# Ten state buffers instead of nine in a fused Mamba and convolution kernel, with the engines' written orders laid out anew

## The chip, the cores and the metric

The kernel runs on one core of a Trainium2 chip. The metric is the device time of one execution in microseconds. Before the change, three runs took 858.09, 858.99 and 859.21 us; the median is 858.99.

## What is computed

The input x has the shape (4, 128, 32, 32), float32. Two Mamba blocks read it as 128 sequences of 32 tokens with 128 features, both in the same memory order. For each block:

```
xc, z  = split(x @ W_in.T)                 # 2 x 256 features
xc     = silu(causal_conv4(xc) + conv_b)
dt,B,C = softplus(W_dt(...) + b_dt), 16 rows B, 16 rows C from W_x(xc)
h[n]   = exp(dt * A[n]) * h[n] + dt * xc * B[n]       # n = 0..15, along the 32 tokens
y      = (sum_n h[n] * C[n] + D * xc) * silu(z)
out    = y @ W_out.T
```

Then y1 + y2 + x goes through batch norm, relu, a 3x3 convolution with binarised weights, batch norm, relu, a second such convolution, and is added to the block's input.

## The kernel before, in words

The tokens are cut into chunks of 512. Four images, two chunks each, two Mambas: 16 items, in each of which the 16 states of the recurrence are worked off one after the other. A state is a tile of 128 partitions x 2 halves x 512 tokens. The whole loop is software-pipelined by hand: each engine has a loop over items k (from -1) and over slots s = 0..15, and at each slot it runs what tables at the top of the file (lines 51 to 96) name. The numbers in the tables are states; 16 and above are states of the next item, and below 0 of the item before. Nothing else orders the work but these tables and semaphores.

One state n passes through these steps:

- A decay exp(dt*A) is made by ScalarE in two halves. Plain states (PLAIN) have it written into one of two pairs of PSUM banks, pair n % 2 (plain_decays, line 654). Turned states (TURNED) have it written into the state's SBUF slot (turned_decays, line 665).
- The input dt*xc*B. For plain states GpSimd multiplies u by a row of B spread over the partitions, into the state's slot (times_b, line 565). For turned states ScalarE makes four products with tokens on partitions (line 678; three such buffers), and TensorE transposes them, eight instructions, into the pair (turn_input, line 1051).
- VectorE scans (line 865). The target is the slot if GpSimd multiplies by C next (POOL_C, line 574), else the pair, and VectorE itself multiplies by C into the slot (DVE_C, line 875).
- TensorE sums the slot into y_sum (line 1058). Then the slot is free.

A pair of banks is free again after the scan two states before, or after VectorE's C product if that state was in DVE_C. A slot is n % SLOTS, and is free once state n - SLOTS is summed (wait_slot_free). The last columns of the slots hold raw weights in the set-up, so some slots also wait for these to be transposed.

In the same slots each engine prepares the next item: TensorE the taps of the causal convolution (PE_TAPS), z (PE_Z), dbc (PE_DBC), dt (PE_DT), the transposes of B and u (PE_B_TOK, PE_U_TOK); ScalarE xc, gate, dbc, dt and copies (ACT_XC and so on), with a load of its function tables in four places; GpSimd u (POOL_U). VectorE gates the sums of the item before inside state 4 (DVE_POST, line 887). From the second image on, the output projection of the image before (PE_OUT, line 1150) is added in (DVE_OUT, line 898) in two items of each image; in the last item, projections are early (AT_EARLY_OUT, AT_EARLY_ADD). The 3x3 kernels are signed, transposed and summed in slots AT_KERNELS of the first item. SyncE issues the loads that spread the rows of B and C (store_rows, spread_b, spread_c).

Below, s4 is the scan of state 4, C4 its C product, B4 and T4 its input by GpSimd or its transposed input, P4 its products, d4 and td4 its decay (plain or turned). Items are counted from 0. The loop is followed by the two convolutions, which run alone.

Of the kernel before, what the change touches and what calls it, by code (L numbers as in the profile page):

```python
# [41 lines left out]
PART = NB * H * PADDED + 2  # L42
WCOUNT = C * C * TAPS

SLOTS = 9
PAIRS = 2
PRODUCTS = 3
FAR = 1e33
# [2 lines left out]

TURNED = (1, 3, 6, 7, 10, 13, 14, 15)
PLAIN = tuple(s for s in range(NST) if s not in TURNED)
POOL_C = (0, 1, 2, 3, 7, 8, 10, 12, 14, 15)
DVE_C = tuple(s for s in range(NST) if s not in POOL_C)
B_GROUPS = ((0,), (2,), (4, 5), (8, 9), (11, 12))
C_GROUPS = tuple((s, s + 1) for s in range(0, NST, 2))

PE_TAPS = {13: ((2, 0),), 14: ((2, 1),), 1: ((1, 2), (1, 3)), 3: ((1, 4), (1, 5), (1, 6), (1, 7))}
PE_OUT = {8: (0,), 10: (1, 2), 11: (3,)}
PE_TURNS = {1: (3,), 4: (6,), 5: (7,), 8: (10,), 11: (13,), 12: (14,), 13: (15,), 15: (17,)}
PE_SUMS = {0: (-4, -3), 2: (-2,), 3: (-1,), 4: (0,), 6: (1, 2), 8: (3, 4), 9: (5,), 10: (6, 7), 11: (8,), 12: (9,),
           13: (10,), 15: (11,)}
POOL_B = {0: (4,), 1: (5,), 5: (8, 9), 8: (11, 12), 12: (16,), 13: (18,)}
ACT_DECAYS = {1: (2,), 3: (4,), 4: (5,), 7: (8,), 8: (9,), 9: (11,), 10: (12,), 15: (16,)}  # L70
ACT_TURNED = {2: (3, 6), 4: (7,), 8: (10,), 9: (13,), 13: (14,), 14: (15, 17)}
ACT_EARLY = {6: (13,), 13: (15,), 15: (17,)}
ACT_PRODUCTS = {3: (7,), 4: (10,), 12: (14,), 15: (19, 22)}
PE_Z = 4
PE_DBC = 6
PE_DT = 7
PE_B_TOK = 9
PE_U_TOK = (11, 12)
ACT_XC = 4
ACT_GATE = 6  # L80
ACT_DBC = 7
ACT_DT = 8
ACT_B_TOK = 12
ACT_U_TOK = (13, 14)
POOL_U = 8

LATE_SUMS = sum(e < 0 for states in PE_SUMS.values() for e in states)
DVE_POST = 4
DVE_OUT = 13

POST_INSIDE = True
AT_KERNELS = (8, 9, 10)
AT_STATS = 8
AT_EXACT = (11, 12)
AT_EARLY_OUT = (5, 6, 8, 9)
# [8 lines left out]
def by_pool(n):  # L104

    return n % NST in POOL_C and n != LAST - 1

# [9 lines left out]
def mamba_conv_kernel(nc, t, out):  # L117
# [3 lines left out]
    with ctx:  # L121
# [10 lines left out]

        state = sb("state", [128, SLOTS, HALVES, CHUNK])
        raw = state[:, :, :, :].rearrange("p a h n -> p (a h n)")
        raw_free = [SLOTS * HALVES * CHUNK]

# [175 lines left out]
        def wait_slot_free(eng, n):  # L312

            wait(eng, summed, n - SLOTS + 1)
            if RAW_SLOT <= n < SLOTS:
                eng.wait_ge(setup_mm, WEIGHT_GROUPS)
# [22 lines left out]
        def tile(n):  # L339
            return state[:, n % SLOTS, :, :]  # L340

# [115 lines left out]
        @block.sync  # L457
        def _(sp):
            load_w_in(sp, 0)
            load_w_x(sp, 0)  # L460
            load_x_tokens(sp, 1)
            load_w_in(sp, 1)
            load_conv_w(sp, 1)
            load_x_tokens(sp, 2)
            load_w_x(sp, 1)
            load_vectors(sp, 1)
            load_w_dt(sp, 1)
            load_a_log(sp, 1)
            for m in range(2):
                load_w_out(sp, m)  # L470

            def load_kernels():

                for n in range(2):
                    sp.dma_start(k_raw[n], t[f"L1_conv_w{n}"].rearrange("o i a b -> o (i a b)")).then_inc(load_k, 16)
                    sp.dma_start(gamma[n][:, :], t[f"L1_conv_gamma{n}"].rearrange("(p a) -> p a", a=1)).then_inc(load_k, 16)
                    sp.dma_start(beta[n][:, :], t[f"L1_conv_beta{n}"].rearrange("(p a) -> p a", a=1)).then_inc(load_k, 16)

            def store_rows(k):

                if k >= 2:
                    for q in range(len(B_GROUPS)):
                        sp.wait_ge(b_loaded[q], 16 * (k - 1))
                    for q in range(len(C_GROUPS)):
                        sp.wait_ge(c_loaded[q], 16 * (k - 1))
                sp.wait_ge(dbc_ready, k + 1)
                sp.dma_start(bc_rows[k % 2], dbc[0:BC, :]).then_inc(rows_stored, 16)
                sp.wait_ge(rows_stored, 16 * (k + 1))

            def spread(wide, first, k, row, count, loaded):  # L490

                sp.dma_start(wide[:, first:first + count, :].rearrange("p s n -> p (s n)"),
                             bc_rows[k % 2][row:row + count, :].rearrange("s n -> (s n)").unsqueeze(0)
                             .to_broadcast([128, count * CHUNK])).then_inc(loaded, 16)

            def spread_b(k, q):

                states = B_GROUPS[q]
                if k > 0:
                    sp.wait_ge(plain_input, before(PLAIN, NST * (k - 1) + states[-1] + 1))  # L500
                spread(b_wide, PLAIN.index(states[0]), k, states[0], len(states), b_loaded[q])

            def spread_c(k, q):

                if k > 0:
                    for s in C_GROUPS[q]:
                        wait_output(sp, NST * (k - 1) + s)
                spread(c_wide, C_GROUPS[q][0], k, NST + C_GROUPS[q][0], len(C_GROUPS[q]), c_loaded[q])

            for k in range(ITEMS):  # L510
                store_rows(k)
                spread_b(k, 0)
                spread_b(k, 1)
                spread_b(k, 2)
                spread_c(k, 0)
                spread_b(k, 3)
                spread_c(k, 1)
                spread_c(k, 2)
                spread_b(k, 4)
                spread_c(k, 3)  # L520
                spread_c(k, 4)
                spread_c(k, 5)
                spread_c(k, 6)
                spread_c(k, 7)
                if k == 0:
                    load_kernels()
                if k % ITEMS_PER_IMAGE == ITEMS_PER_IMAGE - 1:
                    b = k // ITEMS_PER_IMAGE
                    sp.wait_ge(z_mm, 2 * (k + 1))
                    sp.dma_start(res[b], x[b].rearrange("c h w -> c (h w)")).then_inc(load_res[b], 16)  # L530

            for n in range(TILES):
                sp.wait_ge(y_ready, n + 1)
                b, half = n // 2, n % 2
                sp.dma_start(out[b].rearrange("c h w -> c (h w)")[:, half * CHUNK:(half + 1) * CHUNK],
                             res_half(n)).then_inc(y_stored, 16)
            sp.wait_ge(y_stored, 16 * TILES)
# [81 lines left out]
        def _(act):  # L619
# [26 lines left out]
            def plain_decays(n):  # L646

                if n >= LAST or n % NST in TURNED:
                    return
# [18 lines left out]
            def products(n):  # L668
# [3 lines left out]
                k, s = n // NST, n % NST  # L672
                j = before(TURNED, n)
                wait(act, u_tok_ready, 2 * k + 2)
# [13 lines left out]
            def prepare(k, s):  # L688
# [23 lines left out]
                if s == ACT_DT:  # L712
                    act.preload_act_table_set("softplus")  # L713
                    wait(act, plain_decay, HALVES * len(PLAIN) * (k - 1))
                    wait(act, turned_decay, HALVES * len(TURNED) * (k - 1))
                    for h in range(HALVES):
# [538 lines left out]
```

## Time and profile before

| | us |
|---|---|
| median of three runs | 858.99 |
| the profiled execution, its time | 859.51 |
| its span | 857.6 |
| TensorE (PE) busy | 760.1 (89%) |
| VectorE (DVE) busy | 757.2 (88%) |
| ScalarE (ACT) busy | 724.1 (84%) |
| GpSimd (POOL) busy | 710.3 (83%) |

The shares are means over stages with different limits: the set-up until 42.12 us, the loop until about 768.5 us, and the convolutions until the end, where GpSimd does nothing and VectorE and ScalarE wait for TensorE. An instruction's duration is a little more than the distance to the next one's start, since neighbours overlap: a scan lasts 2.26 us. Busy TensorE is not TensorE at its peak.

### The profile page before, as it was taken

To read this page: it belongs to the slowest core of one execution; us is meant where nothing else is said; L and a number is where in the kernel's file an instruction comes from. 1 tells how busy PE (TensorE), PEld (TensorE's weight loads), DVE (VectorE), ACT (ScalarE), POOL (GpSimd) and SP (SyncE) were. 2 spreads that over 40 slices of the span, in tenths; PEclk is the share of its full clock that TensorE was granted. 3 is DMA by queue.
4 is the path that set the end of the run, shared out by engine and by line. 5 is a ranking of instruction groups with operands and counts; after the bars stand their busy time and mean duration, and the time that the engine had idled before them with its cause. 6 is when DMAs were issued, how large, how long until landed. Compare 5 with 4: busy or idle time off the path is not lost.

```text
span 857.6 us, 13007 instructions
## 1 busy us (share of the span) xinstructions
PE 760.1 (89%) x4470; PEld 380.3 (44%) x4470; DVE 757.2 (88%) x482; ACT 724.1 (84%) x1295; POOL 710.3 (83%) x335
## 2 busy tenths in 40 slices
PE   7786989999899999898999998989999986868988
PEld 3533434343445353344353533434534433426866
DVE  2698999999999999999999999999999999984141
ACT  3788999999999999999999999999999999435050
POOL 0477899999999999999999999999999999940000
PEclk9699999999999999999999999999999998898999
DMA  5717143253525151617070717271525244000011
GB/s 141 285 68 249 50 151 148 113 210 105 194 78 216 70 209 48 250 58 265 28 270 26 257 42 248 75 247 50 228 72 195 104 158 165 1 1 1 0 37 62
DMA packets 39146, 110.97 MB, mean 129 GB/s; under 512 B 7244, under 2 KB 9384, under 8 KB 39080
## 3 DMA queue, kind: packets, MB, share of 16 engines
q1 hardware_dynamic: 37724, 109.84, 36.3%
q8 instruction: 36, 0.59, 0.3%
q10 hardware_dynamic: 1356, 0.29, 0.2%
q14 instruction: 30, 0.25, 0.1%
HBM read 106.97 MB, written 3.15 MB: 128 GB/s over the span
## 4 chain that ended last, share of the span: by engine, by line
DVE 33%; issue 20%; ACT 18%; PE 17%; POOL 11%; DMA 0%; ACTq 0%; DVEq 0%; POOLq 0%
DVE state L865 15%; DVE bank L865 12%; PE bank L1225 8%; POOL state L574 5%; ACT bank L654 5%; ACT product L678 5%; POOL state L565 5%; ACT state L665 3%; PE bank L1058 3%; DVE state L875 2%; PE bank L1051 2%; ACT dt L718 1%; ACT L713 1%; PE bank L1037 1%; PE bank L991 1%
## 5 line engine op out<-in xcount | busy, mean ns | idle before, releaser
L574 POOL TENSOR_TENSOR state<-state,wide 128x1024 f32<-128x1024 f32 x159 | 373.0, 2365 | 21.8 <-DVE state L865 21.8
L565 POOL TENSOR_TENSOR state<-u,wide 128x1024 f32<-128x1024 f32 x128 | 301.7, 2369 | 8.2 <-PE bank L1058 8.2
L1058 PE MATMUL bank<-state,ident 64*64 64x512 f32 x2048 | 263.7, 625 | 1.0 <-POOL state L574 0.9
L865 DVE TENSOR_TENSOR_SCAN state<-state,bank 128x1024 f32<-128x1024 f32 x95 | 214.7, 2270 | 1.0 <-PE bank L1051 1.0
L678 ACT ACTIVATE product<-u_tok,b_tok 128x256 f32<-128x256 f32 x512 | 212.4, 496 | 2.3 <-PE bank L1051 1.8
L1051 PE MATMUL bank<-ident,product 128*128 128x128 f32 x1024 | 142.0, 283 | 70.4 <-ACT product L678 26.2
L654 ACT ACTIVATE bank<-dt,a_neg 128x512 f32<-128x512 f32 x256 | 165.5, 677 | 30.4 <-DVE state L865 17.1
L1051 PEld LDWEIGHTS bank<-ident,product 128*128 128x128 f32 x1024 | 114.5, 144 | 166.3 <-issue 91.8
L665 ACT ACTIVATE state<-dt,a_neg 128x512 f32<-128x512 f32 x256 | 166.5, 710 | 0.2 <-PE bank L1058 0.2
L865 DVE TENSOR_TENSOR_SCAN bank<-bank,state 128x1024 f32<-128x1024 f32 x64 | 146.1, 2282 | 1.1 <-ACT bank L654 0.3
L865 DVE TENSOR_TENSOR_SCAN state<-bank,state 128x1024 f32<-128x1024 f32 x64 | 145.2, 2268 | 0.0
L875 DVE TENSOR_TENSOR state<-bank,wide 128x1024 f32<-128x1024 f32 x97 | 118.6, 1223 | 9.3 <-DVE bank L865 1.0
L1037 PE MATMUL bank<-x_t,w_tap 128*128 128x512 f32 x256 | 124.5, 620 | 0.0
L1058 PEld LDWEIGHTS bank<-state,ident 64*64 64x64 f32 x2048 | 67.3, 136 | 114.0 <-issue 107.5
L1225 PE MATMUL bank<-wide 128*128 128x512 f32 (+1 forms) x288 | 71.2, 411 | 8.0 <-ACT u_tok L775 4.0
L865 DVE TENSOR_TENSOR_SCAN bank<-state,bank 128x1024 f32<-128x1024 f32 x33 | 75.2, 2280 | 0.5 <-ACT state L665 0.5
L1037 PEld LDWEIGHTS bank<-x_t,w_tap 128*128 128x128 f32 x256 | 46.1, 194 | 65.3 <-issue 65.3
L1225 PEld LDWEIGHTS bank<-wide 128*128 128x128 f32 x288 | 57.2, 199 | 21.8 <-ACT wide L775 4.4
L587 POOL TENSOR_TENSOR u<-dt,xc 128x1024 f32<-128x1024 f32 x16 | 37.8, 2360 | 25.6 <-ACT dt L718 23.1
L1110 PE MATMUL bank<-dbc,w_dt 8*128 8x512 f32 x64 | 31.7, 613 | 0.5 <-ACT dbc L621 0.5
L1083 PE MATMUL bank<-x_t,w_z 128*128 128x512 f32 x64 | 30.3, 594 | 0.6 <-ACT xc L700 0.6
L1100 PE MATMUL bank<-xc,w_x 128*40 128x512 f32 x64 | 30.6, 600 | 0.0
(93 smaller groups left out, 493.9 us busy)
## 6 DMA issues: line engine op xcount, KB each, us to landing
wide<-bc_rows SPq DMA_DIRECT2D x176, 512.0 KB, 6.8
wide<-bc_rows SPq DMA_DIRECT2D x32, 256.0 KB, 3.6
x_t<-in_x_dram SPq DMA_DIRECT2D x4, 512.0 KB, 4.8
out_dram<-x_t SPq DMA_DIRECT2D x8, 256.0 KB, 2.0
k_room<-in_L_conv_w_dram SPq DMA_DIRECT2D x2, 576.0 KB, 13.0
bc_rows<-dbc SPq DMA_DIRECT2D x16, 64.0 KB, 1.6
state<-in_L_conv_W_in_dram SPq DMA_DIRECT2D x2, 256.0 KB, 3.9
x_tok<-in_x_dram ACTq DMA_DIRECT2D x1, 256.0 KB, 3.7
```

The source lines that it names most:

```text
L565: pool.tensor_tensor(tile(n), u[:, :, :], over_halves(b_wide[:, PLAIN.index(s), :]), ALU.mult).then_inc(plain_input, 1)
L574: pool.tensor_tensor(tile(n), tile(n), over_halves(c_wide[:, n % NST, :]), ALU.mult).then_inc(output_pool, 1)
L587: pool.tensor_tensor(u[:, :, :], dt[m][:, :, :], xc[m][:, :, :], ALU.mult).then_inc(u_ready, 1)
L654: act.activation(pair[n % PAIRS][:, h, :], dt[k % 2][:, h, :], ACT.Exp, scale=a_neg[k % 2][:, h, s:s + 1]).then_inc(plain_decay, 1)
L665: act.activation(tile(n)[:, h, :], dt[k % 2][:, h, :], ACT.Exp, scale=a_neg[k % 2][:, h, s:s + 1]).then_inc(turned_decay, 1)
L678: act.activation(product[j % PRODUCTS][:, blk, :], u_tok[:, blk, :], ACT.Identity, scale=b_tok[k % 2][:, blk, s:s + 1]).then_inc(product_r ...
L865: dve.tensor_tensor_scan(flat(target), flat(decay), flat(source), 0.0, ALU.mult, ALU.add).then_inc(scanned, 1)
L875: dve.tensor_tensor(tile(n), pair[n % PAIRS], over_halves(c_wide[:, s, :]), ALU.mult).then_inc(output_dve, 1)
L1037: mm = pe.matmul(by_sequence(work[h]), w_tap[k % 2][:, h, tap, :], chunk_of(k, tap), start=(tap == 0), stop=(tap == KCONV - 1))
L1051: mm = pe.transpose(pair[n % PAIRS][:, h, 128 * blk:128 * blk + 128], product[j % PRODUCTS][:, blk, 128 * h:128 * h + 128], ident[:, :])
L1058: return pe.matmul(y_sum[64 * h:64 * h + 64, b, :], weights[rows, :], source[rows, h, :], start=first, stop=last)
L1225: mm = pe.matmul(by_row(bank[n])[:, dst, :], k_exact[layer][:, q, :], shifted(part, q)[:, src, 0:W], start=(q == TAP_ORDER[0] and part == ...
```

## The change

SLOTS goes from 9 to 10. The sets of turned states and of states whose C product is GpSimd's are changed; each keeps its size (8 and 10). All tables of orders are rewritten, and one SyncE load is moved.

```diff
-SLOTS = 9
+SLOTS = 10
-TURNED = (1, 3, 6, 7, 10, 13, 14, 15)
+TURNED = (1, 2, 5, 6, 10, 13, 14, 15)
-POOL_C = (0, 1, 2, 3, 7, 8, 10, 12, 14, 15)
+POOL_C = (1, 2, 3, 5, 6, 7, 10, 12, 14, 15)
-B_GROUPS = ((0,), (2,), (4, 5), (8, 9), (11, 12))
+B_GROUPS = ((0,), (3, 4), (7, 8), (9,), (11, 12))
-PE_TAPS = {13: ((2, 0),), 14: ((2, 1),), 1: ((1, 2), (1, 3)), 3: ((1, 4), (1, 5), (1, 6), (1, 7))}
-PE_OUT = {8: (0,), 10: (1, 2), 11: (3,)}
-PE_TURNS = {1: (3,), 4: (6,), 5: (7,), 8: (10,), 11: (13,), 12: (14,), 13: (15,), 15: (17,)}
-PE_SUMS = {0: (-4, -3), 2: (-2,), 3: (-1,), 4: (0,), 6: (1, 2), 8: (3, 4), 9: (5,), 10: (6, 7), 11: (8,), 12: (9,),
-           13: (10,), 15: (11,)}
-POOL_B = {0: (4,), 1: (5,), 5: (8, 9), 8: (11, 12), 12: (16,), 13: (18,)}
-ACT_DECAYS = {1: (2,), 3: (4,), 4: (5,), 7: (8,), 8: (9,), 9: (11,), 10: (12,), 15: (16,)}
-ACT_TURNED = {2: (3, 6), 4: (7,), 8: (10,), 9: (13,), 13: (14,), 14: (15, 17)}
-ACT_EARLY = {6: (13,), 13: (15,), 15: (17,)}
-ACT_PRODUCTS = {3: (7,), 4: (10,), 12: (14,), 15: (19, 22)}
+PE_TAPS = {14: ((2, 0), (2, 1)), 2: ((1, 2), (1, 3), (1, 4), (1, 5), (1, 6), (1, 7))}
+PE_OUT = {9: (0, 1), 12: (2,), 13: (3,)}
+PE_TURNS = {0: (1,), 1: (2,), 3: (5,), 5: (6,), 8: (10,), 12: (13,), 13: (14,), 14: (15,)}
+PE_SUMS = {0: (-2,), 2: (-1,), 5: (0, 1), 6: (2, 3), 8: (4, 5), 9: (6,), 10: (7, 8), 11: (9,), 12: (10,), 13: (11,),
+           15: (12, 13)}
+POOL_B = {1: (7, 8), 5: (9,), 8: (11,), 10: (12,), 11: (16,), 12: (19,), 13: (20,)}
+ACT_DECAYS = {0: (3,), 3: (4,), 5: (7,), 6: (8,), 7: (9,), 8: (11,), 9: (12,), 14: (16,)}
+ACT_TURNED = {0: (5,), 3: (6,), 7: (10,), 9: (13,), 11: (14, 15), 12: (17,), 13: (18,)}
+ACT_EARLY = {0: (6,), 11: (15,), 15: (17, 18, 21)}
+ACT_PRODUCTS = {3: (10,), 6: (13,), 8: (14,)}
-PE_DBC = 6
-PE_DT = 7
-PE_B_TOK = 9
-PE_U_TOK = (11, 12)
-ACT_XC = 4
-ACT_GATE = 6
-ACT_DBC = 7
-ACT_DT = 8
-ACT_B_TOK = 12
-ACT_U_TOK = (13, 14)
-POOL_U = 8
+PE_DBC = 5
+PE_DT = 6
+PE_B_TOK = 11
+PE_U_TOK = (12, 14)
+ACT_XC = 3
+ACT_GATE = 4
+ACT_DBC = 5
+ACT_DT = 7
+ACT_B_TOK = 10
+ACT_U_TOK = (11, 14)
+POOL_U = 10
-DVE_OUT = 13
+DVE_OUT = 14
-AT_KERNELS = (8, 9, 10)
+AT_KERNELS = (9, 10, 11)
@@ the loads of an item, on SyncE
                 spread_c(k, 2)
+                spread_c(k, 3)
                 spread_b(k, 4)
-                spread_c(k, 3)
                 spread_c(k, 4)
```

With these sets VectorE makes the C products of states 0, 4, 8, 9, 11 and 13, where it made those of 4, 5, 6, 9, 11 and 13. PE_Z, DVE_POST, AT_EARLY_OUT and AT_EARLY_ADD are unchanged.

## Rows read from the trace of the kernel before

**Rows 1.** Busy time by stretch: length, busy time (instructions) per engine, TensorE's clock.

```profile
42.12:93.66 51.54, 40.51 (x222) 19.72 (x221) 46.62 (x30) 44.92 (x77) 38.25 (x18) 0.90 0.43 148
93.66:716.32 622.66, 574.81 (x3550) 263.42 (x3548) 613.74 (x343) 604.09 (x1093) 618.78 (x281) 0.98 0.41 146
716.32:768.50 52.18, 36.09 (x264) 17.58 (x264) 49.69 (x34) 29.84 (x56) 42.04 (x21) 0.90 0.06 23
137.79:181.93 44.14, 40.30 (x240) 17.05 (x240) 43.56 (x26) 43.12 (x80) 43.44 (x20) 0.96 0.36 138
```

**Rows 2.** VectorE in one middle item: start, duration, line, operation, shapes.

```profile
139.97 2.26 DVE L865 TENSOR_TENSOR_SCAN state<-state,bank 128x1024 f32<-128x1024 f32 x1
146.51 2.27 DVE L865 TENSOR_TENSOR_SCAN bank<-bank,state 128x1024 f32<-128x1024 f32 x1
151.01 2.29 DVE L865 TENSOR_TENSOR_SCAN bank<-bank,state 128x1024 f32<-128x1024 f32 x1
...
154.54 2.29 DVE L865 TENSOR_TENSOR_SCAN bank<-state,bank 128x1024 f32<-128x1024 f32 x1
```

**Rows 3.** VectorE in the first item; in brackets the idle time before, and its releaser.

```profile
77.51 0.35 DVE L845 COPY k_t<-bank 128x128 bf16<-128x128 bf16 x2 [2.54 <-PE bank L1012]
...
88.97 2.29 DVE L865 TENSOR_TENSOR_SCAN state<-state,bank 128x1024 f32<-128x1024 f32 x1 [0.84 <-PE bank L1051]
```

**Rows 4.** VectorE in the last item.

```profile
725.04 2.27 DVE L865 TENSOR_TENSOR_SCAN bank<-bank,state 128x1024 f32<-128x1024 f32 x1
...
739.58 0.69 DVE L898 TENSOR_TENSOR x_t<-x_t,bank 128x512 f32<-128x512 f32 x1 [0.70 <-PE bank L1150]
...
750.53 0.69 DVE L898 TENSOR_TENSOR x_t<-x_t,bank 128x512 f32<-128x512 f32 x1 [1.17 <-PE bank L1150]
```

**Rows 5.** GpSimd, the multiplications of two neighbouring items that make u.

```profile
257.34 2.36 POOL L587 TENSOR_TENSOR u<-dt,xc 128x1024 f32<-128x1024 f32 x1 [0.17 <-POOL state L565]
...
301.80 2.37 POOL L587 TENSOR_TENSOR u<-dt,xc 128x1024 f32<-128x1024 f32 x1 [0.17 <-POOL state L565]
```

**Rows 6.** ScalarE in one middle item, in order of time.

```profile
148.57 1.32 ACT L665 ACTIVATE state<-dt,a_neg 128x512 f32<-128x512 f32 x2
...
151.21 1.27 ACT L700 ACTIVATE xc<-bank,vectors 128x512 f32<-128x512 f32 x2
...
155.55 1.06 ACT L686 ACTIVATE gate<-bank 128x512 f32<-128x512 f32 x2
...
158.25 1.30 ACT L654 ACTIVATE bank<-dt,a_neg 128x512 f32<-128x512 f32 x2 [0.33 <-DVE state L875]
...
178.06 0.58 ACT L621 ACTIVATE u_tok<-bank 128x512 f32<-128x512 f32 x1
178.67 1.70 ACT L678 ACTIVATE product<-u_tok,b_tok 128x256 f32<-128x256 f32 x4
180.28 1.28 ACT L654 ACTIVATE bank<-dt,a_neg 128x512 f32<-128x512 f32 x2
181.51 3.29 ACT L678 ACTIVATE product<-u_tok,b_tok 128x256 f32<-128x256 f32 x8
```

**Rows 7.** TensorE: transposed inputs in a middle and the last item, then two windows.

```profile
151.23 1.07 PE L1051 MATMUL bank<-ident,product 128*128 128x128 f32 x8 [0.56 <-DVE state L875]
...
729.77 1.94 PE L1051 MATMUL bank<-ident,product 128*128 128x128 f32 x8 [5.91 <-DVE state L875]
...
729.77:733.60 3.83, 3.83 (x20) 2.29 (x24) 3.73 (x3) 1.96 (x5) 3.83 (x3) 0.50 0.00 0
...
163.60:167.20 3.60, 3.60 (x19) 0.81 (x17) 3.50 (x3) 3.56 (x5) 3.13 (x2) 0.53 0.69 264
```

**Rows 8.** ScalarE in the first item: signs of the kernels, first copy of them.

```profile
63.99 2.20 ACT L640 ACTIVATE k_room<-k_room 128x1152 bf16<-128x1152 f32 x2
...
72.54 1.02 ACT L621 ACTIVATE k_t<-bank 128x1024 bf16<-128x1024 bf16 x1
```

**Rows 9.** The page's DMA issues: size, median us from issue to landing.

```profile
wide<-bc_rows SPq DMA_DIRECT2D x176, 512.0 KB, 6.8
```

## The prediction

> **What bounds the kernel now.** I read the windows by stretch first, then VectorE (DVE) in order of time, then who waits for whom. The state loop runs from 42.12 us, where the first scan starts, to 768.5 us: 16 items of 16 states. In its 14 middle items (93.66 to 716.32) DVE is busy 613.74 of 622.66 us, GpSimd (POOL) 618.78 and ScalarE (ACT) 604.09 [rows 1]. Three engines run level, so a gain for one is worth only what it lacks to the next.
>
> DVE has the floor. Inside an item scans start 2.18 us apart (s0 of one item at 137.79, s1 at 139.97); a scan whose C product is also DVE's takes 3.53 (151.01 to 154.54); the state that also holds the gating takes 4.50 (146.51 to 151.01) [rows 2]. An item has ten, five and one of these: 21.80 + 17.65 + 4.50 = 43.95 us. The item of 137.79 took 44.14 [rows 1]. Six of the 14 middle items also add an output (0.60). The floor of the stretch is 14 x 43.95 + 6 x 0.60 = 618.9, so only 3.8 us of its 622.66 are idle. The first item takes 51.54, with visible waits of 2.54 (for the kernel transposes of state 10) and 0.84 (turned input of state 14) [rows 3]; the last takes 52.18 with waits of 0.70 and 1.17 for early output projections [rows 4]. What an order can win is these waits, under 10 us in all.
>
> POOL's own pace: one u to the next, 257.34 to 301.80, is 44.46 us with nothing idle [rows 5]. That is level with DVE's 622.66 / 14 = 44.48.
>
> **The change, counted.** Turned states stay 8, POOL's C products 10, DVE's 6, the table loads, transposes and the loads of rows as many as before (those of B are regrouped, five either way). So no engine gets less work; only waits can go or come. I walk the new orders with the starts of the rows.
>
> *Scans and pairs.* DVE's C set has 0 in place of 5 and 8 in place of 6; state 4 stays in it, so the floor stays 43.95. New starts inside an item, from s0 = 0: s1 3.53, s2 5.71, s3 7.89, s4 10.07, s5 14.57, s6 16.75, s7 18.93, s8 21.11, s9 24.64, s10 28.17, s11 30.35, s12 33.88, s13 36.06, s14 39.59, s15 41.77.
>
> *Middle items, ACT.* A decay of a plain state can start only when the scan two before has left the pair. ACT's run from the next item's d0 (0.17 after s15 starts, as the pair's release comes some 0.1 after a scan's end) to its d7 has no idle place. Steps from the rows: decay 1.23; copy of u and a product 2.22, further products 1.61; a turned decay with a table load 2.64; xc and two products 4.34, so xc alone 1.12; gate with a table load 2.37 (155.55 to 158.25, less the wait of 0.33) [rows 6]. The run is 0.17 + 1.23 (d0) + 2.22 (u, P1) + 4.83 (P2, P5, P6) + 3.69 (d3, td5, d4) + 2.64 (td6, load) + 1.12 (xc) + 1.61 (P10) + 2.37 (gate, load) + 1.30 (d7) + 0.10 (its signal) = 21.28. DVE needs from s15 to s7 2.18 + 18.93 = 21.11. So s7 waits some 0.15 in an item that follows one without an addition; the addition, now between s14 and s15, gives ACT 0.60 and hides it. Eight items x 0.15 = 1.2. With 0.03 per item of uneven starts: 1.7 us where 3.8 are idle today. Term: -2.0. Bounds: -3.8 (no waits at all) and +1.0 (a TensorE transposition late once per plain item by 0.35, see below). I take -2.0, since each step is a row of this same stage.
>
> *Middle items, TensorE and POOL.* The turned inputs must land in 2.1 us between the release of their pair and the scan (states 2, 6, 13, 15), and a transposition takes 1.07 [rows 7]; in the walk the margins are 0.85, 0.6, 0.85 and 0.75, and in items with outputs 0.1 to 0.9. POOL does C5, C6, C7 at 16.2, 18.5, 20.9 plus its lag x; they need s5 to s7 ended, so x is at least 0.57, and B11 must end before 30.35, so x at most 4.8. At 44.46 against DVE's (618.9 + 1.7) / 14 = 44.33 the lag grows by 1.8 in 14 items: POOL stays inside. The tenth slot is what permits B7, B8 at the item's start: they need states 13 and 14 summed, and by nine slots 14 and 15.
>
> *SyncE's queue.* The load of C rows 6 and 7 now stands ahead of that of B rows 11 and 12. It waits for C7 (done at 23.2 + x), the other for B12 (27.9 + x), both long before the next item's use; a load lands in 6.8 us [rows 9]. Cost 0; if C7 were late by a whole product (2.3), the next item's B11, due 25 us after its s0, would still be served. At the start the second B load is twice as large, and its rows are wanted by POOL 2.3 us after the first; a late landing eats only idle time of POOL.
>
> *First item.* s0 stays at 42.12 (setup copies on DVE). C0 moves to DVE, so s1 starts at 45.65. ACT waits for scan 1 to end (47.9) for d3, then its run to d7 ends at 60.9, while s7 would be due at 60.1: about 0.9 lost. The signs of the kernels (2.20 [rows 8]) now stand behind dt, d11 and P14: d7's start at 59.5 + 1.23 + copy 0.5 + d8 1.23 + P13 1.61 + d9 1.23 + 2.64 + dt 1.15 + load 1.3 + d11 1.23 + P14 1.61 = 73.4, signs until 75.6; d12, td13, then the copy of kernel 0 (1.02 [rows 8]) until 79.2; transposes of kernel 1, its copy until 81.6; the sums reach DVE at 82.2. DVE is there at 78.5: the wait is 3.7, not 2.54. But T14 and T15 now have their pairs in time (wait 0.84 and a smaller one go). s0 of the next item comes at 93.5 against 93.66. Term: -0.1; bounds -3.4 (both waits of before gone) and +0.8 (TensorE still slow at T15, as at T14 before). I take -0.1, the walk.
>
> *Last item.* The early projections keep their slots (5, 6, 8, 9) and additions theirs (after s7 and s10). In front of the first addition TensorE runs T6, the skip and sum of 0, then outputs, two sums, outputs. Before, T6 started 4.73 after s4 (725.04 to 729.77) and the addition ran 9.81 later (739.58) [rows 4, 7]. Now T6 waits for the C product of state 4, again 4.73 after s4, which starts at 10.07 and not at 8.72; the work behind it is the same (T7 leaves, sum 3 comes in, both near 1 us). The addition comes at 10.07 + 4.73 + 9.81 = 24.6; DVE is there at 21.1, not 22.6. The wait is 3.5 instead of 0.70. The second addition keeps its distance (T10 waits for C8, but DVE has that product in its path too): 1.2. Term: +2.8. [...]
>
> [...]
>
> **Sum.** -2.0 - 0.1 + 2.8 = +0.7. The profiled execution: span 857.6, its time 859.5; hence 860.2. The median of the runs shown lies 0.5 below that execution, so I predict 859.7. Under 0.2% (1.7 us) a measurement of this kernel can't tell from no change.
>
> **Rivals.**
> - *The first item pays.* The extra slot lets POOL multiply B7 and B8 while it idles today, and the wait for the kernels' sums closes as well: -3.4 instead of -0.1, in all 2.8 - 2.0 - 3.4 = -2.6, and 859.0 - 2.6 = 856.4. For it: POOL's spare time there, and that ACT idles in that item. Against: the signs' place behind dt. Chance 0.28, faster.
> - *POOL sets the pace.* If its lag starts above 4 us, DVE follows at 44.46 per item and the -2.0 falls away: +2.7, 861.7. For it: 618.78 of 622.66 us busy. Against: my walk starts it at 0.6. Chance 0.12, slower.
> - *ACT's run from d0 to d7.* It holds gate, xc and seven decays and products without a gap. If it takes 0.4 more than 21.28, by the gate's wait for z behind a late xc, say, each of the 8 plain items pays it at s7: +3.2, in all +3.9: 862.9. It decides from 21.1 us on (21.7 after an addition). For it: ACT works 43.1 of 44.14 [rows 1]. Against: every step is a row's. Chance 0.20, slower.
>
> The forecast has 0.40. Faster 0.28, same 0.40, slower 0.32. Range: from 856.0 (the first rival, a little beyond) to 863.2 (the last with its price).
>
> **What would show it.** Middle item without addition 44.1 to 44.2, with addition 44.6, and 620 to 621 for fourteen. In the first item a wait of 3 to 4 us for the transposes of the kernels and one near s7. In the last, a wait of 2 to 3.5 us before the first addition. Idle time of POOL between its first B products and C1 near 7.7 us. It is wrong if the 14 items take over 622, or if the wait before the first addition is under 1 us.

## The result and the profile after

The kernel with ten buffers takes 862.30 us (median of 20 executions, 858.36 to 864.59); the kernel before took 858.35 (20 executions, 855.88 to 859.65) beside it. The ratio is 1.0048 [1.0037, 1.0059]: slower by 0.48%. The forecast was 859.7 from a median of 858.99: a sum of +0.7, which it called no measurable change, in a range of 856.0 to 863.2. The time is in the range, but the change is +3.95, clear of the noise and more than five times the sum. The profiled execution took 863.14 us with a span of 861.3 (before: 859.51 and 857.6).

The 20 executions of the kernel after fall into two groups. Four, whose mean granted TensorE clock was 0.966 to 0.974, took 858.36 to 859.47; the other sixteen, at 0.958 to 0.962, took 860.82 to 864.59. The profile is one of the sixteen, and none of the four was kept. So the loss read below is that of most executions, and a part of it comes and goes.

Windows of the kernel after, by stretch: start and end, length, then per engine busy time (instructions) of TensorE, its weight loads, VectorE, ScalarE and GpSimd, then the granted clock.

```profile
42.34:95.64 53.30, 40.44 (x243) 18.96 (x245) 46.92 (x29) 42.49 (x71) 37.23 (x17) 0.94 0.44 150
95.64:717.30 621.66, 568.59 (x3560) 268.07 (x3552) 613.74 (x344) 603.14 (x1093) 618.06 (x281) 0.98 0.43 147
717.30:773.23 55.93, 38.03 (x240) 19.32 (x240) 49.95 (x34) 30.35 (x59) 38.99 (x20) 0.82 0.06 20
773.23:861.30 88.07, 75.34 (x332) 60.35 (x328) 28.46 (x48) 22.91 (x34) 0.00 (x0) 0.95 0.07 24
```

Set against [rows 1]:

| stretch | before | after | difference | predicted |
|---|---|---|---|---|
| until the first scan | 42.12 | 42.34 | +0.2 | 0 |
| first item | 51.54 | 53.30 | +1.8 | -0.1 |
| 14 middle items | 622.66 | 621.66 | -1.0 | -2.0 |
| last item, to the convolutions | 52.18 | 55.93 | +3.7 | +2.8 |
| convolutions | 89.10 | 88.07 | -1.0 | 0 |

The sum is the +3.7 by which the spans differ. VectorE's 613.74 us of work in the middle items is the same to the last digit: no work went, only waits did. The convolutions are the same program; they were granted 0.95 of the clock here and 0.94 before.

Of these differences the -1.0 of the middle items is the least certain, since it is one execution against one. In seven profiles of kernels with the new order (the one after and the runs below that leave these items alone) the 14 items take 621.08 to 623.07 us, 621.7 in the mean; in four with the old order 622.21 to 624.13, 623.2 in the mean. So -1.5 is the better figure. Single items ran longer where the granted clock was lower: in the run with the later additions the item at 137.17 took 45.18 us at 0.92 and the next 44.16 at 1.00; in the kernel after the items of this kind at 139.91, 184.17 and 361.83 took 44.26 to 44.27 at 0.96.

*The first item.* VectorE in the kernel after, in order of time (start, duration, line, operation, shapes, and in brackets the idle time before it with its releaser):

```profile
61.10 2.29 DVE L865 TENSOR_TENSOR_SCAN state<-bank,state 128x1024 f32<-128x1024 f32 x1 [0.55 <-ACT bank L654]
...
77.45 1.23 DVE L875 TENSOR_TENSOR state<-bank,wide 128x1024 f32<-128x1024 f32 x1
83.80 0.36 DVE L845 COPY k_t<-bank 128x128 bf16<-128x128 bf16 x2 [5.12 <-PE bank L1012]
84.07 0.15 DVE L848 TENSOR_SCALAR k_mean<-bank 128x2 f32<-128x2 f32 x1
84.25 1.39 DVE L851 TENSOR_TENSOR k_mean_sq<-k_mean 128x2 f32<-128x2 f32 x1
```

State 7 waits 0.55 for ScalarE's decay. Then VectorE stands 5.12 us until the 3x3 kernels' sums are ready, where [rows 3] had 2.54 in the same place. ScalarE and TensorE of the same stretch:

```profile
73.51 2.20 ACT L640 ACTIVATE k_room<-k_room 128x1152 bf16<-128x1152 f32 x2
...
78.07 1.00 ACT L621 ACTIVATE k_t<-bank 128x1024 bf16<-128x1024 bf16 x1
...
82.06 0.22 ACT L621 ACTIVATE b_tok<-bank 128x64 f32<-128x64 f32 x1 [2.99 <-PE bank L1114]
82.18 1.02 ACT L621 ACTIVATE k_t<-bank 128x1024 bf16<-128x1024 bf16 x1
```

```profile
75.86 1.04 PE L1005 MATMUL bank<-k_room 128*128 128x128 bf16 x8 [5.00 <-ACT k_room L640]
76.83 3.69 PE L1058 MATMUL bank<-state,ident 64*64 64x512 f32 x16
80.45 1.07 PE L1005 MATMUL bank<-k_room 128*128 128x128 bf16 x8
...
83.42 0.34 PE L1012 MATMUL bank<-k_abs,k_room 128*128 128x2 f32 x2
```

TensorE has stood 5.00 us for the signs. From 75.90 to 81.50 it was busy all the time and the window was granted 0.50: the sums of two states (x16) take 3.69 us, where the same group takes 1.95 in a profile that was granted 1.00 there (both edits, below). The low and the high level of the clock are, in what follows, these two, a granted 0.50 and a granted 1.00. The second kernel's transposes start when these sums end, at 80.45, not when the first kernel's copy does, at 79.1. ScalarE's copy of the second kernel (82.18) also stands behind its copy of B (82.06), which waits 2.99 us for TensorE.

*The last item.* VectorE after, the rows that answer to [rows 4], and TensorE ahead of the first addition:

```profile
723.78 2.29 DVE L865 TENSOR_TENSOR_SCAN state<-state,bank 128x1024 f32<-128x1024 f32 x1 [0.69 <-PE bank L1051]
...
737.14 2.27 DVE L865 TENSOR_TENSOR_SCAN state<-bank,state 128x1024 f32<-128x1024 f32 x1
742.94 0.69 DVE L898 TENSOR_TENSOR x_t<-x_t,bank 128x512 f32<-128x512 f32 x1 [3.54 <-PE bank L1150]
...
755.21 0.69 DVE L898 TENSOR_TENSOR x_t<-x_t,bank 128x512 f32<-128x512 f32 x1 [1.13 <-PE bank L1150]
```

```profile
721.71 1.97 PE L1051 MATMUL bank<-ident,product 128*128 128x128 f32 x8
...
728.40 1.94 PE L1051 MATMUL bank<-ident,product 128*128 128x128 f32 x8 [3.70 <-DVE state L865]
732.89 1.94 PE L1051 MATMUL bank<-ident,product 128*128 128x128 f32 x8 [2.56 <-DVE state L875]
734.76 1.99 PE L1058 MATMUL bank<-xc,d_diag 64*64 64x512 f32 x8
```

The wait for the first addition is 3.54 (0.70 before), for the second 1.13 (1.17). A third wait, 0.69 at state 2, is new: T2 is the group at 721.71 and takes 1.97 us at a granted 0.54. T5 (728.40 to 731.00) and T6 with the skip's sum (732.89 to 736.80) were granted 0.50.

*The middle items.* VectorE at states 5, 6 and 7 of an item that follows one without an addition (184.17), and of one that follows one with an addition (273.19):

```profile
198.79 4.46 DVE L865 TENSOR_TENSOR_SCAN state<-state,bank 128x1024 f32<-128x1024 f32 x2
203.28 2.29 DVE L865 TENSOR_TENSOR_SCAN state<-bank,state 128x1024 f32<-128x1024 f32 x1
...
287.76 4.46 DVE L865 TENSOR_TENSOR_SCAN state<-state,bank 128x1024 f32<-128x1024 f32 x2
292.13 2.27 DVE L865 TENSOR_TENSOR_SCAN state<-bank,state 128x1024 f32<-128x1024 f32 x1
```

State 7 starts 4.49 after state 5 in the one and 4.37 in the other: a wait of 0.12, for the decay at the end of ScalarE's run. Items without an addition took 43.97 to 44.27 us, those with one 44.57 to 45.12.

### The profile page after: what moved, and what is told of

Same layout as the page of the kernel before. It is cut to its first block, busy times and chain, and to the rows that moved or that the text cites. A ratio compares the mean times of both kernels' runs of the same rounds, so it can differ in the third digit from the quotient of the medians.

```text
span 861.3 us, 13008 instructions
## 1 busy us (share of the span) xinstructions
PE 754.6 (88%) x4470; PEld 385.0 (45%) x4470; DVE 757.9 (88%) x482; ACT 722.3 (84%) x1295; POOL 710.2 (82%) x335
## 4 chain that ended last, share of the span: by engine, by line
DVE 45%; issue 23%; PE 15%; POOL 9%; ACT 7%; DMA 0%; DVEq 0%; ACTq 0%; POOLq 0%
DVE state L865 23%; DVE bank L865 16%; PE bank L1225 8%; POOL state L574 5%; POOL state L565 4%; DVE state L875 3%; PE bank L1037 2%; ACT state L665 1%; PE bank L1058 1%; ACT bank L654 1%; ACT product L678 1%; PE bank L991 1%; DVE x_tok L887 1%; PE bank L1051 1%; POOL u L587 1%
## 5 line engine op out<-in xcount | busy, mean ns | idle before, releaser
L1058 PE MATMUL bank<-state,ident 64*64 64x512 f32 x2048 | 259.5, 614 | 2.2 <-POOL state L574 2.2
L865 DVE TENSOR_TENSOR_SCAN state<-state,bank 128x1024 f32<-128x1024 f32 x111 | 249.1, 2273 | 0.7 <-PE bank L1051 0.7
L1051 PE MATMUL bank<-ident,product 128*128 128x128 f32 x1024 | 145.6, 288 | 57.3 <-DVE state L875 42.1
L1051 PEld LDWEIGHTS bank<-ident,product 128*128 128x128 f32 x1024 | 119.8, 148 | 145.7 <-issue 103.6
L865 DVE TENSOR_TENSOR_SCAN bank<-bank,state 128x1024 f32<-128x1024 f32 x80 | 182.4, 2280 | 0.0
L1037 PE MATMUL bank<-x_t,w_tap 128*128 128x512 f32 x256 | 119.5, 609 | 2.9 <-DVE x_t L898 2.9
L865 DVE TENSOR_TENSOR_SCAN state<-bank,state 128x1024 f32<-128x1024 f32 x48 | 109.2, 2275 | 0.8 <-ACT bank L654 0.5
L587 POOL TENSOR_TENSOR u<-dt,xc 128x1024 f32<-128x1024 f32 x16 | 37.8, 2363 | 25.8 <-ACT dt L718 23.2
L865 DVE TENSOR_TENSOR_SCAN bank<-state,bank 128x1024 f32<-128x1024 f32 x17 | 38.8, 2280 | 0.0
```

What stands on the lines that cost most here:

```text
L587: pool.tensor_tensor(u[:, :, :], dt[m][:, :, :], xc[m][:, :, :], ALU.mult).then_inc(u_ready, 1)
L865: dve.tensor_tensor_scan(flat(target), flat(decay), flat(source), 0.0, ALU.mult, ALU.add).then_inc(scanned, 1)
L1037: mm = pe.matmul(by_sequence(work[h]), w_tap[k % 2][:, h, tap, :], chunk_of(k, tap), start=(tap == 0), stop=(tap == KCONV - 1))
L1051: mm = pe.transpose(pair[n % PAIRS][:, h, 128 * blk:128 * blk + 128], product[j % PRODUCTS][:, blk, 128 * h:128 * h + 128], ident[:, :])
L1058: return pe.matmul(y_sum[64 * h:64 * h + 64, b, :], weights[rows, :], source[rows, h, :], start=first, stop=last)
```

## The experiments

Theory: the last item pays because VectorE comes earlier to an addition that TensorE cannot serve earlier, and the first because the signs of the kernels stand late and TensorE, which has stood 5.00 us for them, then works at a granted 0.50 (that the standing lowers the clock is my supposition); the middle items give a little, as the walk said. Of the runs, the ratios are to the kernel before, which took 858.14 to 858.37 (medians of 9 to 35 executions).

**The two early additions one slot later** (kernel after).

```diff
-AT_EARLY_ADD = (7, 10)
+AT_EARLY_ADD = (8, 11)
```

> The changed kernel with the two early additions after states 8 and 11 instead of 7 and 10; nothing else. Theory (the last item's additions cost time because VectorE reaches them 3.5 and 1.1 us before TensorE's output projections are ready): the waits of 3.54 and 1.13 us fall under 0.3 each, since VectorE now has 4.1 us more work (state 8 with its C product) before the first. The last item shortens by 4 to 4.6 us and the median falls by about 4, to 858.3. Rival (the wait only moves: what stands behind the additions, the transposition for state 10 and the second pair of projections, is what sets the item's length): both waits go but the scans behind them wait as long, and the time stays within 1 us of the changed kernel's 862.3.

Measured: 857.51 us (12 executions), ratio 0.9994 [0.9983, 1.0006]; 4.8 less than the kernel after. VectorE around the first addition:

```profile
737.07 2.27 DVE L865 TENSOR_TENSOR_SCAN bank<-bank,state 128x1024 f32<-128x1024 f32 x1
739.45 1.23 DVE L875 TENSOR_TENSOR state<-bank,wide 128x1024 f32<-128x1024 f32 x1
740.59 0.68 DVE L898 TENSOR_TENSOR x_t<-x_t,bank 128x512 f32<-128x512 f32 x1
```

The addition now stands behind state 8 and its product and waits for nothing; from the last item's first scan to its last it takes 47.4 us where it took 52.3. The expectation holds, and its rival is out. The waits of the last two additions, after the loop, are 2.7 us in both kernels, so nothing was only moved.

**The same edit in the kernel before.**

> The kernel before with its early additions after states 8 and 11. Theory: its waits of 0.70 and 1.17 us go, the last item shortens by 1.9 us, the ratio to before is 0.997 to 0.999. Rival (VectorE is not what ends that item): ratio 1.000 within 0.0005.

Measured: 856.28 (12), ratio 0.9978 [0.9968, 0.9988]: 2.1 less. The two waits of [rows 4] are worth 1.9. So the same slots cost the new order 4.8 and the old one 2.1: 2.7 us of what the change lost hang on the additions' slots.

**The kernels' transposes earlier in TensorE's and ScalarE's orders, and their sums later** (kernel after).

```diff
-AT_KERNELS = (9, 10, 11)
+AT_KERNELS = (8, 9, 13)
...
-                    pe.wait_ge(k_copied, s - AT_KERNELS[0])
+                    pe.wait_ge(k_copied, AT_KERNELS.index(s))
```

> The changed kernel with the 3x3 kernels' preparation in slots 8, 9 and 13 of the first item instead of 9, 10 and 11: signs right behind dt, the two copies one slot earlier, the last transposes, the sums and VectorE's reading of them behind state 13. Theory (the first item lost 1.8 us because the signs stand behind two more ScalarE steps, and VectorE reads the sums at state 11): VectorE's wait of 5.12 us disappears; the transposition for state 13 comes at 81 to 82 us, so 0.3 to 1.5 us of wait at s13 take its place; item 1 starts at 91.0 to 92.5 instead of 95.64, and the median falls by 3 to 4.5, to about 858.5. Rival (the wait covers other late work, for instance the transposed inputs of states 14 and 15 or GpSimd's products for the next item, which would hold VectorE next): item 1 still starts at 94 or later.

Measured: 860.94 (10), ratio 1.0032 [1.0019, 1.0045]; only 1.4 less, and the two intervals overlap. The wait for the sums fell from 5.12 to 0.24, but another came:

```profile
81.71 2.30 DVE L865 TENSOR_TENSOR_SCAN bank<-state,bank 128x1024 f32<-128x1024 f32 x1 [2.99 <-PE bank L1051]
...
85.57 0.35 DVE L845 COPY k_t<-bank 128x128 bf16<-128x128 bf16 x2 [0.24 <-PE bank L1012]
```

State 13 waits 2.99 us for its transposed input, which is queued behind the kernels' transposes and the sums of two states (1.07 and 3.69 us again, at a granted 0.50 from 74 to 79 us). What the expectation took for a freed wait was shared with the next thing in TensorE's queue. The next item does start at 92.12, inside what was expected, but only because the first scan came early (39.78, not 42.34; the set-up is the same code): the first item takes 52.34 where it took 53.30, which is the rival's side.

**Both edits.**

> The changed kernel with both earlier edits: additions after states 8 and 11, kernels in slots 8, 9 and 13. Theory (the two places are independent and add): the additions gave 4.6 us and the kernels' slots about 1.4, so the median is 856 to 857 and the ratio to before 0.997 to 0.999. Rival (with TensorE's phases shifted the late transposition at state 13 eats the second gain): within 0.5 us of the first edit alone, 857.5.

Measured: 856.84 (11), ratio 0.9986 [0.9975, 0.9997]; 5.5 less than the kernel after, where the two alone give 4.8 and 1.4. It is 0.7 less than with the additions alone, and those two intervals overlap: what the kernels' slots give is small, and not shown clear of the noise. In this profile the same TensorE code ran at a granted 1.00 from 74 to 79 us, and the wait at state 13 is 0.47:

```profile
74.11 0.70 PE L1005 MATMUL bank<-k_room 128*128 128x128 bf16 x8 [1.94 <-ACT k_t L621]
74.74 1.95 PE L1058 MATMUL bank<-state,ident 64*64 64x512 f32 x16
```

```profile
79.20 2.29 DVE L865 TENSOR_TENSOR_SCAN bank<-state,bank 128x1024 f32<-128x1024 f32 x1 [0.47 <-PE bank L1051]
```

Nothing in the first item differs between these two kernels, and ScalarE's starts agree to 0.02 us until 76.4; TensorE had stood 3.04 us for the signs in both, and was granted 0.50 after it in the one (70.49 to 72.00) and 1.00 in the other (70.47 to 72.10). What differs is the clock, and with it go the 2.5 us at state 13. At the high level this first item takes 49.84 us, 1.7 less than before.

**TensorE kept busy while it waits** (kernel after). Extra matmuls whose results nobody reads, in the first item ahead of the wait for the signs, and in slots 2 and 3 of the last. One wait is added, for a dt that was made in the item before.

```diff
+FILL_FIRST = 4
+FILL_LAST = {2: 3, 3: 2}
...
+            def fill(calls):
+                for _ in range(calls):
+                    pe.matmul(work[0][:, :], w_tap[0][:, 0, 0, :], w_tap[0][:, 0, :, :].rearrange("p k e -> p (k e)"))
...
                     pe.wait_ge(dt_ready, HALVES + 1)
+                    fill(FILL_FIRST)
                     pe.wait_ge(k_signed, 2)
...
+                    if k == ITEMS - 1 and s in FILL_LAST:
+                        wait(pe, dt_ready, HALVES * ITEMS)
+                        fill(FILL_LAST[s])
```

> The changed kernel with idle TensorE kept busy in two places by matmuls whose result nobody reads: four 128x512 ones in the first item while it waits for the signs of the kernels, three and two in the last item before the transpositions for states 5 and 6. No other edit. [...] Together 3 us less, a median near 859.5. Rival (the order alone makes the waits, the clock is incidental): both waits stay within 0.5 us of 5.12 and 3.54.

Measured: 860.30 (12), ratio 1.0025 [1.0012, 1.0038]; 2.0 less, with more work. Its lines are 2 (VectorE) and 8 (TensorE) higher. TensorE in the first item and at T6 and the skip's sum of the last:

```profile
74.18 0.71 PE L1013 MATMUL bank<-k_room 128*128 128x128 bf16 x8 [1.28 <-ACT k_room L642]
74.82 1.95 PE L1066 MATMUL bank<-state,ident 64*64 64x512 f32 x16
...
730.96 1.06 PE L1059 MATMUL bank<-ident,product 128*128 128x128 f32 x8 [1.71 <-DVE state L877]
731.95 1.09 PE L1066 MATMUL bank<-xc,d_diag 64*64 64x512 f32 x8
```

```profile
80.38 0.35 DVE L847 COPY k_t<-bank 128x128 bf16<-128x128 bf16 x2 [3.29 <-PE bank L1020]
...
738.95 0.69 DVE L900 TENSOR_TENSOR x_t<-x_t,bank 128x512 f32<-128x512 f32 x1 [1.59 <-PE bank L1158]
```

1.95 in place of 3.69, 1.06 in place of 1.94, 1.09 in place of 1.99. The wait for the kernels' sums becomes 3.29 (3.3 to 3.8 were expected), the one before the first addition 1.59 (1.6 to 2.2). TensorE was granted 1.00 in both stretches (69 to 79 us and 729 to 735), so these are the waits at the high level: the first near the 3.7 of the prediction, the second 1.95 below the 3.54 at the low level. Of the two waits' 8.66 us, 3.8 (1.83 and 1.95) go with the clock. Only 2.0 of them show in the time, where 3 were expected. That the extra matmuls are what kept the clock up is not shown by one profile: with both edits the stretch from 66 to 79 us was granted 1.00 without them. In this profile the second addition waits 1.73 and not 1.13, and the 14 middle items take 623.07 and not 621.66; two scans there wait 0.6 and 0.9 us for transposed inputs.

**The diagonal of the second Mamba made by ScalarE** (kernel after). Before the first scan VectorE writes two diagonals, which take 4.66 us beside GpSimd's products (the last section has the rows), and TensorE's transposes of x stand for VectorE's next copy (w_out).

```diff
                                 setup_copy(act, copy, g, setup_act)
+                        act.wait_ge(twin_ready, 2)
+                        act.wait_ge(*copied(11))
+                        act.wait_ge(diag_ready, HALVES)
+                        for h in range(HALVES):
+                            act.activation(d_diag[1][:, h, :], ident2[:, :], ACT.Identity,
+                                           scale=d_skip[1][:, h:h + 1]).then_inc(diag_ready, 1)
...
-            skip_diagonal(1)
             copies(GROUPS_AT_B_TOK)
```

> The changed kernel with the two set-up diagonals of the second Mamba written by ScalarE instead of VectorE. In all profiles VectorE's diagonal takes 0.25 us while GpSimd is idle, and 2.39 each while GpSimd multiplies; the first scan follows VectorE's set-up work. Theory (VectorE and GpSimd exclude each other there, and VectorE is the chain to the first scan): the first scan starts 3.5 to 4.6 us earlier against the same set-up phase (37.8 to 38.8 where it was 42.3), ScalarE adds 0.5, and the median falls by 2 to 4 to about 859. Rival (transposes of x or the first decay hold the first scan anyway): it starts less than 1 us earlier, no change in the median.

Measured: 859.31 (12), ratio 1.0015 [1.0003, 1.0027]; 3.0 less. TensorE in the kernel after, then in this one:

```profile
36.26 5.31 PE L991 MATMUL bank<-ident,x_tok 128*128 128x128 f32 x24 [2.08 <-DVE w_out L455]
```

```profile
33.67 5.11 PE L996 MATMUL bank<-ident,x_tok 128*128 128x128 f32 x24
```

The first scan starts at 39.42, not 42.34; 37.8 to 38.8 were expected. That start is no evidence by itself, since one set-up code gave 39.77 to 42.34 in different executions. But here the two set-ups are alike: their first eight matmuls of the causal convolution take 5.97 and 5.88 us. Where these take 3.70, the diagonal moves the first scan from 39.77 (both edits) to 37.84 (both and the diagonal, below).

**Nine buffers under the new order**, and **ten under the old one**.

```diff
-SLOTS = 10
+SLOTS = 9
```

> The changed kernel with nine state buffers again and all new orders kept. Theory (the buffer itself is worth little: the B products of states 7 and 8 then wait for the sums of states 14 and 15 of the item before, which comes out as GpSimd being 1 to 2 us later against VectorE, inside the window of about 4 us that it has): the 14 middle items take 621 to 623 us, as with ten, and the median stays within 1.5 us of the changed kernel's. Rival (the tenth buffer is what carries the new order): GpSimd idles in each item, an item takes 45 to 46 us, and the time rises by 10 us or more.

> The kernel before with ten state buffers and none of the new orders. Theory (in it only GpSimd waits for a buffer, 8.2 us, nearly all in the first and last item, and no other engine waits for GpSimd there): these waits of GpSimd shrink, VectorE's do not, and the median stays within 0.1% of before, 857.5 to 859.2. Rival (the buffers bound the start of the loop, so the buffer alone is worth 2 us or more): below 856.5. Second rival (moving everything behind the states by 4 KB per partition costs by itself): above 860.

Measured: nine buffers in the kernel after take 908.82 us (5), ratio 1.0572 [1.0551, 1.0593]; ten in the kernel before 858.14 (11), ratio 0.9999 [0.9989, 1.0009]. The first expectation's theory fell: 46.5 us more than the kernel after, where 1.5 at most were expected; its rival holds. The second's theory holds. Groups of the page of the nine-buffer run (busy time, mean ns, and the idle time before them with what ended it):

```profile
L565 POOL TENSOR_TENSOR state<-u,wide 128x1024 f32<-128x1024 f32 x128 | 300.1, 2362 | 60.2 <-PE bank L1058 59.8
L1058 PE MATMUL bank<-state,ident 64*64 64x512 f32 x2048 | 268.1, 629 | 37.4 <-POOL state L574 37.4
L865 DVE TENSOR_TENSOR_SCAN state<-state,bank 128x1024 f32<-128x1024 f32 x111 | 249.5, 2274 | 29.5 <-PE bank L1051 29.3
...
L865 DVE TENSOR_TENSOR_SCAN bank<-bank,state 128x1024 f32<-128x1024 f32 x80 | 182.6, 2283 | 14.1 <-POOL state L565 14.1
```

and of the kernel after, the first of these:

```profile
L565 POOL TENSOR_TENSOR state<-u,wide 128x1024 f32<-128x1024 f32 x128 | 300.3, 2362 | 4.7 <-PE bank L1058 4.6
```

GpSimd's input products now wait 59.8 us for TensorE to sum the state whose slot they need, mostly B9, which with nine slots needs state 0 of the same item summed; TensorE in turn waits 37.4 for GpSimd, and VectorE's scans 29.3 and 14.1 for the two. A middle item takes 45.4 to 49.1 us. So the tenth buffer alone gives nothing, and the order alone loses 46 us: neither is a part that can be had by itself.

**Two edits that were to gain more.** The base is the kernel after with three of the edits above (additions, kernels, diagonal).

> The changed kernel with three edits together: additions after states 8 and 11, kernels in slots 8, 9 and 13, second Mamba's diagonals by ScalarE. Theory (three separate places on VectorE's path): 862.3 - 4.6 - 1.4 - 3.0 = 853.3, in between 852.5 and 855 since the kernels' slots gave 0.7 to 1.4; ratio to before 0.994 to 0.996. Rival (an earlier first scan meets ScalarE or GpSimd unready in the first item, and its gain is lost there): 856 or more.

Measured: 853.99 (5), ratio 0.9951 [0.9939, 0.9964]: 8.3 below the kernel after, as expected. In its profile state 13 waits 2.46 us again; its transposed input ends only at 78.73, with TensorE at a granted 0.70 from 74 to 79 us; the first item takes 51.42 where it took 49.84.

Then the four products of state 10 moved behind the decay of state 7 in ScalarE's order, to take the 0.12 us from state 7:

```diff
-ACT_PRODUCTS = {3: (10,), 6: (13,), 8: (14,)}
+ACT_PRODUCTS = {5: (10,), 6: (13,), 8: (14,)}
```

> As a_bd, and the four products of state 10 made after the decay for state 7 instead of before the gate. Theory (in an item that follows one without an addition, VectorE's scan of state 7 waits 0.12 us for ScalarE's run from the decay of state 0 to that of state 7, in which these products hold 1.6 us): the distance of scans 6 and 7 becomes 2.18 in all middle items where it is 2.30 in eight, the 14 items shorten by 0.8 to 1.2 us, and the median by about 1. Rival (GpSimd, busy 618 of 621.7 us there, sets the pace once this wait is gone): the 2.30 become 2.18 and other scans get the time back; the 14 items stay within 0.3 us.

Measured: 862.47 (5), ratio 1.0049 [1.0037, 1.0062]; 8.5 more, not less. ScalarE and VectorE in this kernel (lines 5 to 8 higher):

```profile
193.13 1.26 ACT L700 ACTIVATE xc<-bank,vectors 128x512 f32<-128x512 f32 x2
195.09 0.60 ACT L686 ACTIVATE gate<-bank 128x512 f32<-128x512 f32 x1 [0.70 <-PE bank L1088]
195.89 0.60 ACT L686 ACTIVATE gate<-bank 128x512 f32<-128x512 f32 x1 [0.20 <-PE bank L1088]
```

```profile
202.51 2.30 DVE L870 TENSOR_TENSOR_SCAN bank<-bank,state 128x1024 f32<-128x1024 f32 x1 [0.69 <-ACT bank L654]
```

The wait at state 7 went, as expected. But the products had stood between xc and gate and covered the time in which TensorE makes z out of xc (1.99 us, from 193.87). Without them ScalarE stands 0.90 us for z, and the products, done later, push the decay of state 8: a wait of 0.69 there, in nearly every item (9.2 us in the whole loop). The 14 middle items take 630.77 us, where the base took 621.11. This is the mechanism that the prediction's third rival named, the gate's wait for z, one state later than it said.

> As a_bdp, and three matmuls without a use on TensorE in the first item, while it waits for the signs of the kernels. [...] Rival (the clock is high there in most executions anyway): within 0.5 us of a_bdp.

Measured, with three extra matmuls in the first item on top: 861.96 (5), ratio 1.0047 [1.0034, 1.0059], not to be told from the run before it, where up to 1.5 us less were expected. In the two profiles the first item takes 50.98 us and 52.59, but the times do not show it.

**The kernel before with the two edits that apply to it** (additions one slot later, the diagonal on ScalarE).

> The kernel before with additions after states 8 and 11 and the second Mamba's diagonals by ScalarE. Theory: the diagonals are worth the same 2.9 us here as in the changed kernel, since the set-up is the same: 856.3 - 2.9 = 853.4, ratio 0.994 to 0.996. Rival (here d0 and the products of state 1 come at the end of ScalarE's set-up, and hold the first scan): 855 or more. Against a_bd it says which set of orders is the better base once the three places are mended: by the middle items alone (621.7 against 622.7) the changed one, by 1 us.

Measured: 854.33 (5), ratio 0.9954 [0.9941, 0.9968]. This equals the best version with ten buffers (853.99) within the intervals; that the new order would be 1 us better, as the expectation had it from the middle items, is not shown. The diagonal gives 2.0 here, against 2.9 from both edits to all three.

## Why the time came out in the predicted range, and the sum too small

- *Last item, +2.8: right in mechanism; it measured +3.7.* Wait before the first addition 3.5 predicted, 3.54 measured; second 1.2 and 1.13. What it lacked is T2's wait of 0.69, with TensorE at a granted 0.54.
- *First item, -0.1: this is the term that was mis-sized; it measured +1.8, outside its own bounds (-3.4 and +0.8).* ScalarE's walk held (signs predicted 73.4 to 75.6, though the steps as written add up to 73.2; measured 73.51 to 75.6; the wait at state 7 predicted 0.9, measured 0.55). The walk then priced TensorE's part with lengths of the high level ("transposes of kernel 1, its copy until 81.6"), while it had put the signs so late that TensorE stands 5.00 us in front of it. The wait came out 5.12, not 3.7; the run that fills the idle time, granted 1.00 there, gives 3.29. The walk also left out that ScalarE's second copy stands behind its copy of B. Of the 1.9 us that the term missed, the wait is 1.4 and k_mean_sq 0.6 (1.39 against 0.81), and the smaller wait at state 7 gives 0.35 back. In the last item the low level was in the term from the start, since part of the 9.81 it took over was measured at a granted 0.50 (729.77 to 733.60 [rows 7]); here it was left out, with an upper bound (+0.8) that looked at T15 alone (T14 had taken 1.94 before, at a granted 0.50 from 82.46 to 84.20).
- *Middle items, -2.0: measured -1.0 in the two profiles, -1.5 in the means of all.* The wait at state 7 appears in the items and at the size predicted (0.15; 0.12 measured). The rest of the distance to 620.6 is 1.0 us of waits that no walk of mine had, such as 0.46 us before the C product of state 9 in the item at 406.09. Their cause stays open. A slow stretch in an item is not in the sum; it goes with 1.0 us in the item of 45.18 above, which was granted 0.92.
- *GpSimd's idle time before C1*, predicted 7.7: 7.76. It never set the pace; that rival is out. *The first rival* (the first item pays 3.4) is out: the spare time of GpSimd was not what that item waits for.
- *The tenth buffer.* The prediction said what it permits (B7 and B8 early) and did not price going without: 46 us.
- *The range was partly luck.* Its upper end, 863.2, is the price of the third rival, ScalarE's run from d0 to d7, and that did not come in this kernel. 862.30 lies inside for another reason, the two ends of the loop.

So the loop's measured terms are -1.0 + 1.8 + 3.7, and the change is slower. What it loses is at the two ends of the loop, and is won back by where the additions stand (4.8 us) and perhaps a little by where the kernels' work does, not by the buffer: with both edits the kernel after is at 0.9986 [0.9975, 0.9997]. The old order with its own edits reaches the same time as the new one. That the new order has no net advantage left is measured; that no order of this kind has one is not.

## What to carry to other kernels

Where three engines run level, a new order is worth the waits it removes in the steady stage, so the ends of the loop decide its sign: walk the first and the last item with the same care, and after moving an engine's work forward look for what it meets earlier (here an addition placed by slot, not by readiness). Price TensorE's work near the ends of the loop at both levels of its clock. In this case it was granted 0.50 after 5.91 us of idle time in the last item before [rows 7] and after 5.00 in the first item after, but after 3.04 it was granted 0.50 in one profile and 1.00 in another, and the window at 163.60 has 0.53 with TensorE busy 3.60 of 3.60 us [rows 7]: idle time alone does not tell which level comes. And do not credit an edit with a difference between two profiles before the same code has been seen in more than one. Work that looks as if it only fills an engine's time may be the cover of another engine's latency; ask what the next instruction waits for before moving it.

## What the runs showed of the hardware

*A small VectorE instruction can take as long as GpSimd's large one beside it.* VectorE in the set-up of the kernel after, and GpSimd in the same stretch:

```profile
23.27 0.41 DVE L812 TENSOR_SCALAR d_diag<-ident,vectors 128x64 f32<-128x64 f32 x2
...
29.09 2.21 DVE L804 TENSOR_SCALAR a_neg<-a_neg 128x32 f32<-128x32 f32 x2
31.21 4.66 DVE L812 TENSOR_SCALAR d_diag<-ident,vectors 128x64 f32<-128x64 f32 x2
```

```profile
28.82 11.64 POOL L565 TENSOR_TENSOR state<-u,wide 128x1024 f32<-128x1024 f32 x5
```

The same instruction takes 0.25 us while GpSimd stands (23.27), and 2.3 to 2.4 while it multiplies. The first three of GpSimd's five products, 2.35 each and 2.33 apart, end at 31.17, 33.5 and 35.8; the two diagonals end at 33.5 and 35.87. Each lasts until the GpSimd instruction beside it ends. So does k_mean_sq (128x2): 0.81 us in the kernel before, 1.39 in the one after and 1.80 with the kernels' slots moved. It ends at 78.78, 85.64 and 87.83, and GpSimd's product at 78.76, 85.62 and 87.81 (85.44 + 2.37). Why VectorE's instruction lasts that long the traces do not show. Moving the two diagonals to ScalarE, 0.59 us there for both, took 3.0 us from the kernel.

*TensorE's clock differs between executions of one code.* The wait at state 13 was 2.99 us in one execution and 0.47 in another, with nothing changed in that item; from 74 to 79 us the granted clock was 0.50 in the first and 1.00 in the second. The set-up differs too: eight matmuls of the causal convolution took 5.97 us in the kernel after and 4.46 in the same code of the run with the later additions, whose first scan came 2.2 us earlier (40.14 against 42.34). The profile grants 1.00 there in both (8.9 to 15.0 us and 8.7 to 13.2), so that this too is the clock is my estimate from the lengths (a median of 1.06 us for one matmul against 0.59), and not shown. From the last scan to the end, the same code took 91.67 us in the kernel after and 95.39 with both edits, at a granted 0.96 and 0.91. One profiled execution can so stand 2 us off the next in the set-up, the same again in the first item, and 3.7 at the end; what is under that was read from medians. The mean clock of an execution does not tell where its slow stretches lay: with the extra matmuls four executions at 0.974 to 0.976 took 860.43 to 861.19 us, where the kernel after took 858.36 to 859.03 at 0.974.
